# First attention: the order of transposes and product with v within a round

## The reference

```
H, DH = 16, 64
q = (x @ Wq); k = (x @ Wk); v = (x @ Wv)          # x is the normalized input, 16 heads of 64
scores = q @ k.T * DH**-0.5 + slope[h] * (i - j)   # i: row, j: column
scores = where(j <= i, scores, -1e30)              # causal
attn = softmax(scores, axis=-1)
out = (attn @ v).reshape(b, n, H * DH)
return out @ Wo + bo
```

## Time and profile before

| | |
|---|---|
| median of 3 runs | 5696.39 us (5695.09 to 5696.55) |
| profiled execution, its time | 5695.29 us |
| profiled execution, its span | 5693.5 us |
| TensorE busy | 4098.7 us (72% of the span) |
| VectorE busy | 4586.6 us (81%) |
| ScalarE busy | 4554.9 us (80%) |

### The profile page before, as it was taken

One profiled execution on the slowest core, in us unless ns is written; L12 is line 12 of the kernel. 1 busy time (PEld: TensorE's weight loads), 2 busy tenths in 40 slices (PEclk: granted clock), 3 DMA queues, 4 the chain that ended last, 5 costly groups with the idle time before them and its releaser, 6 DMA issues. The chain is left out here.

```text
span 5693.5 us, 68825 instructions
## 1 busy us (share of the span) xinstructions
PE 4098.7 (72%) x22020; PEld 1821.6 (32%) x22020; DVE 4586.6 (81%) x6913; ACT 4554.9 (80%) x3648; POOL 1429.7 (25%) x1258
## 2 busy tenths in 40 slices
PE   8999999999999999855555555555555555555547
PEld 4555555555555555511111111111111111011105
DVE  6666666666666666799999999999999999999966
ACT  5655555655555556589999999999999999999993
POOL 0000000000000000044444444444444444444420
PEclk9999999999999999966667666667676667776768
DMA  1000000000000000289999999999999999989881
GB/s 40 5 6 5 6 5 5 5 5 5 5 6 6 7 3 1 80 210 187 198 191 194 189 194 189 194 189 195 189 195 188 193 194 188 198 185 198 184 189 64
DMA packets 149375, 639.46 MB, mean 112 GB/s; under 512 B 32662, under 2 KB 74840, under 8 KB 79064
## 3 DMA queue, kind: packets, MB, share of 16 engines
q0 software_dynamic: 73728, 536.90, 47.1%
q1 hardware_dynamic: 75224, 97.37, 5.2%
HBM read 70.22 MB, written 27.13 MB: 17 GB/s over the span
## 5 line engine op out<-in xcount | busy, mean ns | idle before, releaser
L1502 DVE SCALAR_TENSOR_TENSOR b_tiles<-b_ra_rep,b_cap,psum 128x1024 f32<-128x1024 f32 x1024 | 1262.0, 1273 | 55.6 <-PE psum L1768 52.9
L1768 PE MATMUL psum<-b_qT,b_kT 126*128 126x512 bf16 x2048 | 813.6, 508 | 670.3 <-DVE b_tiles L1502 667.0
L679 DVE CUSTOM_DVE_ANT_0 a_srow<-psum,a_bias 128x512 f32<-128x512 f32 (+3 forms) x1280 | 728.6, 608 | 642.2 <-PE psum L860 637.6
L738 ACT ACTIVATE a_pT<-psum 128x512 f32<-128x512 f32 (+3 forms) x1280 | 603.4, 533 | 558.7 <-PE psum L872 558.5
L1781 PE MATMUL psum<-b_tiles,b_v_aug 128*32 128x512 f32 x2752 | 525.2, 849 | 487.0 <-ACT b_tiles L1682 487.0
L1509 DVE TENSOR_SCALAR b_tiles<-b_tiles 128x2048 f32<-128x2048 f32 x512 | 762.4, 1489 | 4.6
L872 PE MATMUL psum<-ident,a_srow 128*128 128x128 f32 x4352 | 626.0, 281 | 42.6 <-ACT a_pT L738 36.0
L860 PE MATMUL psum<-a_k,a_q 64*128 64x512 f32 (+3 forms) x2560 | 623.5, 572 | 0.2
L1682 ACT ACTIVATE b_tiles<-b_tiles,b_sc 128x8192 f32<-128x8192 f32 (+1 forms) x87 | 620.9, 7136 | 2.9
L1768 PEld LDWEIGHTS psum<-b_qT,b_kT 126*128 126x128 bf16 x2048 | 156.6, 110 | 1455.9 <-DVE b_tiles L1502 1094.9
L756 ACT ACTIVATE a_srow<-a_srow,a_nmax 128x1536 f32<-128x1536 f32 (+15 forms) x512 | 611.1, 1203 | 6.1 <-DVE a_nmax L685 5.9
(11 more groups left out here) (221 smaller groups left out, 5124.2 us busy)
## 6 DMA issues: line engine op xcount, KB each, us to landing
b_tiles<-b_tiles POOLq DMA_DIRECT2D x344, 1024.0 KB, 13.1
X<-b_tiles POOLq DMA_DIRECT2D x168, 1024.0 KB, 12.9
b_ra_rep<-ra_scratch SPq DMA_DIRECT2D x32, 1024.0 KB, 9.9
row_scratch<-b_tiles SPq DMA_DIRECT2D x6, 2048.0 KB, 16.4
b_qk_raw<-row_scratch SPq DMA_DIRECT2D x31, 304.0 KB, 2.8
b_v_raw<-row_scratch SPq DMA_DIRECT2D x31, 136.0 KB, 8.6
X<-in_x_dram SPq DMA_DIRECT2D x8, 512.0 KB, 6.6
a_wqk<-in_wqk_dram SPq DMA_DIRECT2D x32, 128.0 KB, 2.7
```

The costliest lines, as they stand in the source:

```text
L679: nc.vector.tensor_tensor_reduce(out=srow[:, n % ROWS, h, a:z], in0=bank(c % 2 * 2 + h, 0, z - a), in1=bias[:, h, off + a:off + z], scale= ...
L1502: nc.vector.scalar_tensor_tensor(out=a[:, s * HALF:(s + 1) * HALF], in0=ra_rep[:, j, s * HALF:(s + 1) * HALF], scalar=cap[:, j, k:k + 1], ...
L1768: last = nc.tensor.matmul(half_ps(s)[:, i * BANK:(i + 1) * BANK], kT[:, j, k * P:(k + 1) * P], qT[:, j, cs], start=True, stop=True)
```

## The change

In each round of a step the group of transposes comes ahead of the part of the product with v. Nothing else is edited.

```
--- before.py
+++ after.py
@@ -411,7 +411,7 @@
             seq += s[i:i + 1]
             if i == 0 and n >= 5 and n % 2:
                 seq += [("O", k)]
-            seq += a[i:i + 1] + t[i:i + 1]
+            seq += t[i:i + 1] + a[i:i + 1]
             if n < 2 and i % 2:
                 seq += [("V", 2 * n + i // 2)]
```

## The result

The changed kernel takes 5746.8 us (median of 4 runs, 5745.74 to 5747.32) beside 5696.09 us before: a ratio of 1.0089, 95% interval 1.0073 to 1.0105. 5749 was forecast, in a range of 5728 to 5768, with 0.95 for slower.

The account below looks back on a forecast made before the run. TensorE was taken to set the pace of every step with a product part. Per head pair 1.90 + 0.60 + 0.61 - 0.45 + 0.62 = 3.28 us, times 16 is 52.5 us: 5749 us beside the median, range 5728 to 5768.

Parts of the forecast that it names:

- What bounds the stage: First attention: TensorE sets the pace of every step with a product part; only its queue changes.
- The sum: All terms for one head pair: 3.28 us slower, times 16 pairs is 52.5 us.
- (a): Last groups of steps 4, 8 and 12: transposes wait for copies held by the product, 3 x 0.63 = 1.90 us.
- (b): First group's head 1 transposes wait for VectorE's scaling: 0.10 us in step 4, 0.50 in step 8.
- (c): ScalarE's lag delays the next odd step: 0.15 us in step 9, 0.23 each in 5 and 13; sum 0.61.
- (d): Steps 6, 10 and 14: last two product parts touch, saving one block entry and exit of 0.15 us each: -0.45.
- (e): Steps 15 and 16: late output block, then transposes waiting for scaling delay product and projection: 0.52 + 0.10 = 0.62 us.
- R1: Rival, faster: held copies are hidden anyway, and step 16's transposes fill its wait; -15 us, 5681 us, chance 0.03.
- R2: Rival: only (a) and (d) count, small delays are taken up elsewhere; 23 us slower, 5719 us, chance 0.07.
- R3: Rival: every transpose group behind another in an even step waits, nine instead of three; 113 us slower, 5809 us, chance 0.05.
- R4: Rival: no measurable change, (a) being smaller and balanced by (d); chance 0.02.

Follow-up runs that it names:

- Taking the hold away: Changed kernel, but ScalarE's copies of even row tiles go to a spare tile, with one memset of pT added; 5715.23 us, ratio 1.0035 to the kernel before.
- the swap where nothing waits: Kernel before, with transposes ahead of the product only in rounds after the first that have scores; 5685.44 us, ratio 0.9982.

## Why the prediction was right, point by point

**What bounds the stage.** Right: TensorE sets the pace in steps 4 to 16, and the pair grew by what its waits and the joined parts add up to. The change is one of TensorE's queue alone but for one exponential of step 16 (below).

**The sum.** 3.28 us per head pair were forecast; the third shows 3.03, and the fourteen usual ones 2.93 to 3.03. Two pairs that the sum took to be like the rest made up for it: the last one (5.2 us) and the one that crosses the batches (3.58). All sixteen together are 50.7 us. Another 0.45 lie ahead of the first pair and 0.9 behind the attention. The start of the first pair differs by up to 1.6 us among the kernels without the memset (42.79 to 44.41), so these two may be scatter. The span grew by 52.0 us, and 52.5 was forecast: part of that closeness is chance.

**(a) Held copies without an S behind them.** Right in mechanism: 0.63 each was forecast, and 0.54 to 0.55 measured in each of steps 4, 8 and 12 (1.13 to 1.14 for the block instead of 0.59). The term was mis-sized by the release: I took 0.20 between the next block's start and the copy from C, a copy of another kind, and this copy starts 0.11 after (410.29 against 410.18). Taking the hold away and swapping only the last rounds confirm the mechanism from two sides.

**(b) Transposes ahead of the scaling.** Right, and a little small: 0.60 was forecast, 0.80 measured. Step 8 lost 0.57 against 0.50, since 0.13 and not 0.05 us pass between the end of L658 and the transpose. In step 4 the block starts at 361.69 and the product at 362.88, 0.17 more than before, where 0.10 was forecast. Step 6 loses 0.06, which I had at nothing.

**(c) The late O.** Too large: 0.61 was forecast for three steps, 0.12 measured in step 9 (1.18 against 1.06) and about 0.4 for the three. The same 0.09 of release would make the difference in steps 5 and 13. Steps 7 and 11 lost nothing, as forecast.

**(d) Parts side by side.** Right: 2.68 became 2.53. The experiment with the swap where nothing waits shows this gain alone. The Trainium skill ("TensorEngine Tiling (Array Packing)", Key Properties) says that changes of tiling mode drain the engine. The gain from fewer blocks is real here, 0.15 us each; that the drain is its cause was not tried. The whole change loses, since it buys three such savings per pair with 3.5 us of waits.

**(e) Steps 15 and 16.** Right: 0.62 was forecast, 0.52 measured up to P's start and about 0.1 in the P block. O was 0.25 late where 0.33 was forecast. Step 16 alone shows that the waits for the scaling take the place of the wait for the copies.

**What was wrong.** I had costed all 16 pairs alike. From the last pair's first matmul to the attention's last, 125.97 us became 131.15: 5.2 more, not 3.0. The runs divide most of the extra 2.2. With step 16 alone swapped the last pair grows by 1.60 where a usual one grows by 0.38. With the rounds with scores swapped it is 0.93 against 0.16, and with only the last rounds swapped 0.97 against 0.96. So most of the extra lies where transposes come early for their scaling. The trace shows why. In the last pair VectorE takes statistics of the finished rows for the next stage (L83, 0.75 us) between its addition and the scaling, which a usual pair does not:

```profile
2293.21 0.69 DVE L699 TENSOR_TENSOR X<-psum,X 128x512 f32<-128x512 f32 x1 [0.73 <-PE psum L901]
2293.94 0.75 DVE L83 BATCH_NORM_STATS2 ln_stats<-X 128x6 f32<-128x256 f32 x2
...
2294.79 0.35 DVE L658 TENSOR_SCALAR a_srow<-a_srow,a_zinv 128x256 f32<-128x256 f32 x1
...
2295.20 0.90 PE L872 MATMUL psum<-ident,a_srow 128*128 128x128 f32 x4 [1.37 <-DVE a_srow L658]
```

The wait for the scaling is 1.37 there instead of 0.59. The crossing pair has the same statistics. Its growth beyond the others is in step 12: the first transposes take 1.41 us instead of 1.03, and the last ones, which ran on into the transposes of the next batch's input as one block, are now parted from them by the product. No run tried that alone.

"VectorE and ScalarE do nothing at the letter A ... so their own queues stay as they are" does not hold in step 16 either. There ScalarE issues its second exponential ahead of the second entry of the list, and the second entry was T and is now A. So the exponential moved behind the held copies. In 15 pairs the projections follow, and no wait shows. In the last pair the copy C comes behind it:

```profile
2297.87 0.66 ACT L738 ACTIVATE a_pT<-psum 128x256 f32<-128x256 f32 x2 [3.08 <-PE psum L890]
2298.41 0.40 ACT L756 ACTIVATE a_srow<-a_srow,a_nmax 128x128 f32<-128x128 f32 x1
...
2298.80 0.38 ACT L738 ACTIVATE a_oT<-psum 128x256 f32<-128x256 f32 x1
```

By these rows C starts 0.39 later for it (2298.80 against 2298.41), an estimate, as no run has that move alone.

**The rivals.** R1 (copies hidden anyway) fell at the block of 1.13. R2 (small delays taken up elsewhere) fell at the waits for L658 and for C, which stand in TensorE's own queue. R3 (every group waits) fell at the rounds with scores, where held copies add no wait. R4 (no measurable change) fell with the measured ratio.

## What to carry to other kernels

Before two blocks in the queue of the bounding engine are swapped, ask of both what each releases: the block that moved back here, the product, was what freed the place that the helpers' copies write, so feeding them sooner made the bank ring the bound. A ring of three holds up its writer only where less work lies between two uses than the helper's answer takes, so look for the rounds at the end of a loop where a block is missing, and swap only the others. And where a queue must wait, put work there that depends on neither side: here it gained as much as the best reordering (10.7 us beside 10.2). Check that on the first and the last trip of each loop too, for the trips that do extra work were the ones that the forecast had wrong.

## What the runs showed of the hardware that was not expected

A GpSimd memset held up VectorE for about its whole length. In the run with the freed copies, VectorE's two scalings of the bias, both SBUF to SBUF in fp32, took 9.04 us instead of 2.48 when the memset of pT ran beside them (timelines of VectorE and of GpSimd of that run):

```profile
4.49 9.04 DVE L633 TENSOR_SCALAR a_bias<-a_ahead,a_slope 128x2048 f32<-128x2048 f32 x2 [4.49 <-POOL a_ahead L616]
...
4.34 6.93 POOL L618 MEMSET a_pT<- 128x8192 f32 x1
```

The first of the two took 7.85 us and the other 1.27. The memset had begun first and was over at 11.27, and the longer one ended about 1.1 after it, at 12.3. The Trainium skill ("SBUF — State Buffer", Who interferes with whom) has the two engines share a port pair as an exclusive lock that the one behind waits for in full, and the trace agrees: the delay of 6.6 us is about the memset's length, not a share of it.
